# Splitting one attention product into high and low parts in a fused attention and expert kernel

## Chip, cores and metric

One core of one Trainium2 chip. The time is the device time of one execution in microseconds, the median of several runs.

## What is computed

For x of shape (8, 512, 128), in float32:

```python
def _L0_attn_ref(x, gamma, beta, w_qkv, w_out, b_out):
    xn = (x - mean) / jnp.sqrt(var + EPS) * gamma + beta
    q, k, v = jnp.split(jnp.einsum('bnc,ck->bnk', xn, w_qkv), 3, axis=2)   # 4 heads of 32
    q = q * DIM_HEAD ** (-0.5)
    k = jax.nn.softmax(k, axis=1)
    context = jnp.einsum('bnhd,bnhe->bhde', k, v)
    out = jnp.einsum('bhde,bnhd->bnhe', context, q)
    return jnp.einsum('bnk,kc->bnc', out.reshape(b, n, 128), w_out) + b_out + x

x = x + _layernorm(_L0_attn_ref(_layernorm(x), ...))
x = x + _layernorm(_L0_ffn_ref(_layernorm(x), Wg, Wu, Wd))
# ffn: sum over 8 experts of (silu(x @ wg) * (x @ wu)) @ wd, hidden size 512
```

## The kernel before

A batch is 512 tokens of 128 channels. The expert part of a batch has 8 experts times 4 blocks of 128 hidden units, 32 **steps**. `body(b)` on every engine walks through the 32 steps of batch b: TensorE makes the gate product, the up product and the down product of three steps earlier (`LAG`); ScalarE the silu `gs` and the high part `h_hi` of h; VectorE `h = gs * up` and the low part `h_lo = h - h_hi`. Each product is float32 accuracy out of three fp32r matmuls of 512 columns (`products`, L1203 to L1206): high by high, low by high, high by low. Gate and up accumulators are three banks each, so a step's h may lag some steps.

The attention of the next batch c = b + 1 is threaded into those steps, and the first part of that of b + 2 too (its normalised rows `xh` and their transpose). Where each piece stands is a table written by hand: `PE_AT`, `DVE_AT`, `ACT_AT` and `POOL_AT` give the step on TensorE, VectorE, ScalarE and GpSimd, and on each engine a piece stands in front of that step's own work, in the middle, or at its end (`FRONT`, `MIDDLE`). Batch 0 has a prologue of its own and its body uses the `FIRST_` tables; batch 1's attention, made in body 0, uses other code (`first`). The engines run their queues in order and meet through semaphores.

The pieces around the change, in the body b for batch c = b + 1:

- step 1: the keys `kT`; step 2: their maximum, the exponentials `ET`, and `E_T`, a transpose within 32x32 blocks. SyncE stores this to DRAM and loads it back in another order (L458, L463) into `t_out_E`, in four loads.
- step 8 on TensorE: **A**, the product of the exponentials with `xh`: four float32 matmuls of 128 columns (L1249), `xh` stationary. It waits for the four loads alone.
- step 9: VectorE evicts A into `A_sb`, scaled by gamma (L897), ahead of that step's h. Just before it makes `erec`, the reciprocal of the exponentials' sum (L891). TensorE makes **B** from it behind that step's down product (L1255). Steps 10 and 11: M and G in the same way; step 12: the attention's output.
- step 6, at its end, on VectorE: `next_stats`, the mean and variance of the input of b + 2 (L860, L845, L856, L850, L852). GpSimd takes the power (`next_rstd`, L504, step 7) and makes `xh` of b + 2 (`next_xn`, L529, step 10, after A has read the old one).
- step 13 to 15: final statistics and scale of batch b - 1; GpSimd adds the residual into `res` (L541, step 15). Steps 16 and 17 on VectorE: transpose of `xh`, the sum `z` and its statistics.

There are 8 bodies; those with `nxt` (b < 6) prepare batch b + 2.

```python
                if at == "A":

                    pe.wait_ge(s_t_load["E"], c * 64)
                    for j in range(J):
                        last = pe.matmul(att_ps[:, 0:D].rearrange("p (i r) -> p i r", r=32), xh[:, j, :],
                                         from_group(t_out["E"][:, :])[:, j], start=(j == 0), stop=(j == J - 1))
                    last.then_inc(s_A_ps, 1)
```

Of the kernel before, what the change touches and what calls it, by code (L numbers as in the profile page):

```python
# [5 lines left out]
ALU = mybir.AluOpType  # L6
# [6 lines left out]
P = 128  # L13
# [17 lines left out]
             "x1_stats": 20, "x1n_T": 24, "next_xnT_lo": 28, "x1n_lo": 31}  # L31
FIRST_ACT = {"E_store": 5, "E_load": 8, "G": 14, "wk_hi": 18, "next_xnT": 26, "next_xnT_hi": 27, "x1n_hi": 30}
FIRST_POOL = {"y": 2, "yb": 6, "next_rstd": 10, "next_xn": 13, "z_rstd": 17, "x1": 17, "x1_rstd": 21}
PE_AT = {"kT": 1, "A": 8, "B": 9, "M": 10, "G": 11, "attn": 12}
DVE_AT = {"kmax": 2, "acc": 2, "E_T": 2, "next_stats": 6, "A": 9, "B": 10, "M": 11, "G": 12, "fin_stats": 13, "fin_scale": 14,
          "z_T": 13, "next_T": 16, "z": 17, "z_stats": 17, "x1_stats": 21, "next_xnT_lo": 23, "x1n_T": 24, "x1n_lo": 31}
ACT_AT = {"exp": 2, "G": 12, "next_xnT": 21, "next_xnT_hi": 22, "x1n_hi": 30}
POOL_AT = {"yb": 4, "next_rstd": 7, "next_xn": 10, "fin_rstd": 13, "fin_out": 15, "z_rstd": 18, "x1": 18, "x1_rstd": 21}

# [41 lines left out]
def build(nc, x, gamma, beta, w_qkv, w_out, b_out, Wg, Wu, Wd, out):  # L81
# [10 lines left out]
    with ctx:  # L92
# [75 lines left out]
        turned = ("x", "E", "x1n", "acc")  # L168
        t_blk = {k: sb(f"t_blk_{k}", [P, N]) for k in turned}
        t_out = {k: sb(f"t_out_{k}", [P, N]) for k in turned}  # L170
# [329 lines left out]
        def _(pool):  # L500
# [66 lines left out]
            def body(b, par, first, nxt, last):  # L567
                for s in range(STEPS):
                    for at, when in (FIRST_POOL if first else POOL_AT).items():
                        if when != s:  # L570
                            continue
                        if at == "fin_rstd":
                            power("fin", b, s_rstd["fin"], s_mv["fin"])
                        elif at == "fin_out":
                            finish(b - 1, 1 - par)
                        elif at == "next_rstd":
                            if nxt:
                                attention("x_rstd", b + 2, par)
# [67 lines left out]
        def _(act):  # L646
# [5 lines left out]
            def attention(at, c, par, first):  # L652
                if at == "next_xnT":
# [187 lines left out]
        def _(dve):  # L841
# [25 lines left out]
            def attention(at, c, par, first):  # L867
# [10 lines left out]
                if at == "wk_lo":  # L878
                    dve.wait_ge(s_wk_hi, 1)
# [320 lines left out]
        def _(pe):  # L1200
# [324 lines left out]
```

## Time and profile before

| | |
|---|---|
| median of 3 runs | 543.82 us (543.82 to 544.1) |
| span of the profiled execution | 541.9 us |
| busy: TensorE, its weight loads | 99%, 86% |
| busy: VectorE, ScalarE, GpSimd | 81%, 64%, 31% |

The profile is of one execution. Its span runs from the first to the last instruction, 541.9 us; its own time outside the span is not given apart from the runs, and the median lies 1.9 us above the span. A row of the timeline has start, duration, engine, line, operation, output <- inputs, the tile of TensorE used, and partitions x elements; "x8" merges eight in a row, and brackets give idle time and what ended it. PE is TensorE's matmuls, PEld its weight loads, DVE VectorE, ACT ScalarE, POOL GpSimd. Matmuls overlap, so their spacing and not their duration says what they cost; a float32 matmul shows as two records.

### The profile page before, as it was taken

The page shows a single profiled execution, that of the slowest core. Times are in us where ns is not written, and L with a number is a line of the kernel's source. Part 1 is how long each engine was busy: PE and PEld are TensorE (multiplying, and loading weights), DVE is VectorE, ACT ScalarE, POOL GpSimd, SP SyncE. Part 2 cuts the span into 40 slices and gives each one's busy share as a digit, 9 for nine tenths or more (in the row PEclk, how much of TensorE's full clock was granted, in tenths as well). Part 3 has the DMA queues.
Part 4 walks back from the last instruction along what each step waited for, and adds up shares of the span by engine and source line. Part 5 has one row for each costly group of instructions (what it writes and reads, how often), then busy time and mean ns, then how long its engine had stood idle before and what let it go on. Part 6 is the DMA issues. An engine that isn't in the chain of part 4 may idle for free.

```text
span 541.9 us, 8650 instructions
## 1 busy us (share of the span) xinstructions
PE 535.4 (99%) x2582; PEld 466.4 (86%) x2582; DVE 441.5 (81%) x965; ACT 348.7 (64%) x633; POOL 167.7 (31%) x217
## 2 busy tenths in 40 slices
PE   9999999999999999999999999999999999999996
PEld 6788888888888888888888888888888888888886
DVE  6896877899777997879977898688987799777866
ACT  5986877557674575855667576665767555655555
POOL 6797950217102280114602045021530016000101
PEclk9999999999999999999999999999999999999999
DMA  7253111120120201202102112021111110110000
GB/s 218 82 169 109 53 59 46 33 72 26 60 72 8 93 25 39 79 19 79 51 9 79 40 59 59 4 75 39 60 39 48 31 60 0 41 39 1 20 2 19
DMA packets 33797, 28.68 MB, mean 53 GB/s; under 512 B 3411, under 2 KB 25686, under 8 KB 33750
## 3 DMA queue, kind: packets, MB, share of 16 engines
q1 hardware_dynamic: 32736, 27.47, 16.1%
q10 hardware_dynamic: 1014, 0.66, 0.4%
q8 instruction: 20, 0.33, 0.3%
q14 instruction: 27, 0.22, 0.1%
HBM read 17.37 MB, written 10.75 MB: 52 GB/s over the span
## 4 chain that ended last, share of the span: by engine, by line
PE 98%; ACT 1%; issue 0%; DVE 0%; POOLq 0%; POOL 0%; DVEq 0%
PE acc_att_ps L1203 11%; PE acc_att_ps L1206 11%; PE acc_att_ps L1204 11%; PE gate_ps L1203 10%; PE gate_ps L1206 10%; PE gate_ps L1204 10%; PE up_ps L1203 10%; PE up_ps L1206 10%; PE up_ps L1204 10%; PE acc_att_ps L1249 1%; PE up_ps L1320 1%; ACT xh L792 0%; PE acc_att_ps L1264 0%; PE acc_att_ps L1261 0%; PE acc_att_ps L1255 0%; PE acc_att_ps L1435 0%
## 5 line engine op out<-in xcount | busy, mean ns | idle before, releaser
L730 ACT ACTIVATE gs<-gate_ps 128x512 f32<-128x512 f32 x255 | 152.1, 597 | 172.8 <-PE gate_ps L1206 170.9
L1006 DVE TENSOR_TENSOR h<-gs,up_ps 128x512 f32<-128x512 f32 x231 | 157.7, 683 | 76.5 <-PE up_ps L1206 66.9
L993 DVE TENSOR_TENSOR h_lo<-h,h_hi 128x512 fp32r<-128x512 f32 x231 | 171.9, 744 | 0.1
L707 ACT ACTIVATE h_hi<-h 128x512 fp32r<-128x512 f32 x231 | 144.0, 624 | 6.4 <-DVE h L1006 5.2
L1203 PE MATMUL gate_ps<-x1nT_hi,wg_hi 128*128 128x512 f32 (+1 forms) x254 | 98.4, 387 | 0.0
L1203 PE MATMUL acc_att_ps<-h_hi,wd_hi 128*128 128x512 f32 (+1 forms) x256 | 96.8, 378 | 0.0
L1206 PE MATMUL acc_att_ps<-h_lo,wd_hi 128*128 128x512 f32 (+1 forms) x256 | 96.8, 378 | 0.0
L1204 PE MATMUL acc_att_ps<-h_hi,wd_lo 128*128 128x512 f32 (+1 forms) x256 | 96.8, 378 | 0.0
L1204 PE MATMUL gate_ps<-x1nT_hi,wg_lo 128*128 128x512 f32 (+1 forms) x254 | 96.1, 378 | 0.0
L1206 PE MATMUL gate_ps<-x1nT_lo,wg_hi 128*128 128x512 f32 (+1 forms) x254 | 96.1, 378 | 0.0
L1203 PE MATMUL up_ps<-x1nT_hi,wu_hi 128*128 128x512 f32 (+1 forms) x254 | 96.1, 378 | 0.0
L1204 PE MATMUL up_ps<-x1nT_hi,wu_lo 128*128 128x512 f32 (+1 forms) x254 | 96.1, 378 | 0.0
L1206 PE MATMUL up_ps<-x1nT_lo,wu_hi 128*128 128x512 f32 (+1 forms) x254 | 96.1, 378 | 0.0
L510 POOL TENSOR_TENSOR rstd_fin<-mv_fin,expo 128x4 f32<-128x4 f32 (+1 forms) x9 | 8.6, 955 | 173.1 <-DVE mv_fin L845 140.3
L1206 PEld LDWEIGHTS acc_att_ps<-h_lo,wd_hi 128*128 128x128 f32 x256 | 48.4, 189 | 7.2
L1204 PEld LDWEIGHTS acc_att_ps<-h_hi,wd_lo 128*128 128x128 f32 x256 | 48.4, 189 | 6.8
L1203 PEld LDWEIGHTS acc_att_ps<-h_hi,wd_hi 128*128 128x128 f32 x256 | 48.4, 189 | 6.8
L1204 PEld LDWEIGHTS up_ps<-x1nT_hi,wu_lo 128*128 128x128 f32 x254 | 48.0, 189 | 6.8
L1203 PEld LDWEIGHTS up_ps<-x1nT_hi,wu_hi 128*128 128x128 f32 x254 | 48.0, 189 | 6.8
L1206 PEld LDWEIGHTS up_ps<-x1nT_lo,wu_hi 128*128 128x128 f32 x254 | 48.0, 189 | 6.8
L1206 PEld LDWEIGHTS gate_ps<-x1nT_lo,wg_hi 128*128 128x128 f32 x254 | 48.0, 189 | 6.7
L1204 PEld LDWEIGHTS gate_ps<-x1nT_hi,wg_lo 128*128 128x128 f32 x254 | 48.1, 189 | 6.0
(263 smaller groups left out, 555.3 us busy)
## 6 DMA issues: line engine op xcount, KB each, us to landing
w_raw<-in_L_ffn_Wg_dram SPq DMA_DIRECT2D x8, 256.0 KB, 3.2
w_raw<-in_L_ffn_Wu_dram SPq DMA_DIRECT2D x8, 256.0 KB, 3.0
w_raw<-in_L_ffn_Wd_dram SPq DMA_DIRECT2D x8, 256.0 KB, 3.3
x_in<-in_L_attn_x_dram SPq DMA_DIRECT2D x7, 256.0 KB, 2.9
t_dram_x1n<-t_blk_x1n SPq DMA_DIRECT2D x7, 256.0 KB, 2.0
t_out_x1n<-t_dram_x1n SPq DMA_DIRECT2D x28, 64.0 KB, 2.0
t_dram_acc<-t_blk_acc SPq DMA_DIRECT2D x7, 256.0 KB, 2.3
t_out_acc<-t_dram_acc SPq DMA_DIRECT2D x28, 64.0 KB, 2.1
```

The lines of the kernel that those rows point to most:

```text
L510: pool.tensor_tensor(rstd[k][:, 0, toks], mv[k][:, toks, 1], expo[:, toks], ALU.pow).then_inc(done, 1)
L707: act.activation(h_hi[s % NH][:, :], h_of(t, s)[:, :], ACT.Copy).then_inc(s_hhi, 1)
L730: act.activation(gs[q][:, :], gate_ps[q][:, :], ACT.Silu).then_inc(s_silu, 1)
L993: dve.tensor_tensor(h_lo[s % NH][:, :], h_of(t, s)[:, :], h_hi[s % NH][:, :].bitcast(F32), ALU.subtract).then_inc(s_hlo, 1)
L1006: dve.tensor_tensor(h_of(t, s)[:, :], gs[q][:, :], up_ps[q][:, :], ALU.mult).then_inc(s_h, 1)
L1203: pe.matmul(ps, w_h, x_h, start=start, stop=False)
L1204: pe.matmul(ps, w_l, x_h, start=False, stop=False)
L1206: return pe.matmul(ps, w_h, x_l, start=False, stop=stop)
L1249: last = pe.matmul(att_ps[:, 0:D].rearrange("p (i r) -> p i r", r=32), xh[:, j, :], from_group(t_out["E"][:, :])[:, j], start=(j == 0), st ...
L1320: pe.matmul(ps[:, 0:cols].rearrange("p (a b) -> p a b", b=P), warm[:, :], warm[:, :].rearrange("p (a b) -> p a b", a=1).to_broadcast([P, c ...
```

## The change

For batches 2 to 7, `xh` and the exponentials are split into high and low parts in fp32r, as the expert products are. A becomes four matmuls of 256 columns, `xh_hi` by the high and low exponentials side by side, and four of 128 columns, `xh_lo` by the high exponentials, accumulated onto the first 128 columns. The other 128 columns are added in the eviction, which becomes two VectorE instructions.

The new pieces: `E_hi` (ScalarE copy, end of step 6, waits for the four loads), `E_lo` (VectorE subtraction, end of step 6), `next_xh_hi` (ScalarE copy, end of step 15), `next_xh_lo` (GpSimd subtraction, step 17). `next_stats` moves from step 6 to step 8, `next_rstd` from 7 to 9, `next_xn` from 10 to 11. To make room, four tiles of the output stage (`t_blk` and `t_out` of the accumulator, `fn`, `res`) and the new `A_hi` go into `w_raw`, the weights' staging tile, free after batch 0; the prologue's `wvT_bd` goes into `zn`. `s_wk_hi` is renamed `s_hi` and also counts `xh_hi`.

```diff
-FIRST_ACT = {"E_store": 5, "E_load": 8, "G": 14, "wk_hi": 18, "next_xnT": 26, ...}
+FIRST_ACT = {"E_store": 5, "E_load": 8, "G": 14, "wk_hi": 18, "next_xh_hi": 24, "next_xnT": 26, ...}
+FIRST_POOL = {..., "x1_rstd": 21, "next_xh_lo": 25}
-DVE_AT = {"kmax": 2, "acc": 2, "E_T": 2, "next_stats": 6, "A": 9, "B": 10, ...}
+DVE_AT = {"kmax": 2, "acc": 2, "E_T": 2, "E_lo": 6, "next_stats": 8, "A": 9, "B": 10, ...}
-ACT_AT = {"exp": 2, "G": 12, "next_xnT": 21, "next_xnT_hi": 22, "x1n_hi": 30}
-POOL_AT = {"yb": 4, "next_rstd": 7, "next_xn": 10, "fin_rstd": 13, "fin_out": 15, "z_rstd": 18, ...}
+ACT_AT = {"exp": 2, "E_hi": 6, "G": 12, "next_xh_hi": 15, "next_xnT": 21, "next_xnT_hi": 22, "x1n_hi": 30}
+POOL_AT = {"yb": 4, "next_rstd": 9, "next_xn": 11, "fin_rstd": 13, "fin_out": 15, "next_xh_lo": 17, "z_rstd": 18, ...}
...
+        def E_part(i):
+            return E_parts[:, :].rearrange("p (b h q) -> p h b q", b=2, h=2)[:, i]
...
+                if at == "xh_lo":
+                    pool.wait_ge(s_hi, c)
+                    pool.tensor_tensor(xh_lo[:, :, :], xh[:, :, :], xh_hi[:, :, :].bitcast(F32),
+                                       ALU.subtract).then_inc(s_xh_lo, 1)
...
+                if at == "next_xh_hi":
+                    act.wait_ge(s_xh, c)
+                    act.wait_ge(s_A_ps, c - 1)
+                    act.activation(xh_hi[:, :, :], xh[:, :, :], ACT.Copy).then_inc(s_hi, 1)
+                if at == "E_hi":
+                    act.wait_ge(s_t_load["E"], c * 64)
+                    act.wait_ge(s_A_ps, c - 1)
+                    act.activation(E_part(0), two(t_out["E"][:, :]), ACT.Copy).then_inc(s_E_hi, 1)
...
+                if at == "E_lo":
+                    dve.wait_ge(s_E_hi, c - 1)
+                    dve.tensor_tensor(E_part(1), two(t_out["E"][:, :]), E_part(0).bitcast(F32),
+                                      ALU.subtract).then_inc(s_E_lo, 1)
...
-                        dve.tensor_scalar(A_sb[:, :], att_ps[:, 0:D], gb_cols[:, 0:1], None, ALU.mult).then_inc(s_A, 1)
+                        dve.tensor_scalar(two(A_hi), blocks_first(att_ps[:, 0:D]), gb_cols[:, 0:1], None, ALU.mult).then_inc(s_A, 1)
+                        dve.wait_ge(s_A, 2 * c - 2)
+                        dve.scalar_tensor_tensor(out=two(A_sb[:, :]), in0=blocks_first(att_ps[:, D:2 * D]), scalar=gb_cols[:, 0:1],
+                                                 in1=two(A_hi), op0=ALU.mult, op1=ALU.add).then_inc(s_A, 1)
...
+                if at == "A" and not first:
+                    pe.wait_ge(s_hi, c)
+                    pe.wait_ge(s_xh_lo, c - 1)
+                    pe.wait_ge(s_E_lo, c - 1)
+                    for j in range(J):
+                        pe.matmul(att_ps[:, 0:2 * D], xh_hi[:, j, :],
+                                  E_parts[:, :].rearrange("p (b x j r) -> p j x r b", b=2, j=J, r=32)[:, j],
+                                  start=(j == 0), stop=False)
+                    for j in range(J):
+                        last = pe.matmul(att_ps[:, 0:D], xh_lo[:, j, :],
+                                         E_part(0).rearrange("p b (a j r) -> p j a r b", j=J, r=32)[:, j],
+                                         start=False, stop=(j == J - 1))
+                    last.then_inc(s_A_ps, 1)
```

**TensorE, step 8 of body 1**, before and in the change:

```order
L1204 MATMUL acc_att_ps<-h_hi,wd_lo 128x512
L1206 MATMUL acc_att_ps<-h_lo,wd_hi 128x512
L1249 MATMUL acc_att_ps<-t_out_E,xh 128x128 x4
L1203 MATMUL gate_ps<-x1nT_hi,wg_hi 128x512
L1204 MATMUL gate_ps<-x1nT_hi,wg_lo 128x512
L1206 MATMUL gate_ps<-x1nT_lo,wg_hi 128x512
```

```order
L1245 MATMUL acc_att_ps<-h_hi,wd_lo 128x512
L1247 MATMUL acc_att_ps<-h_lo,wd_hi 128x512
L1292 MATMUL acc_att_ps<-E_parts,xh_hi 128x256 x4
L1296 MATMUL acc_att_ps<-E_parts,xh_lo 128x128 x4
L1244 MATMUL gate_ps<-x1nT_hi,wg_hi 128x512
L1245 MATMUL gate_ps<-x1nT_hi,wg_lo 128x512
L1247 MATMUL gate_ps<-x1nT_lo,wg_hi 128x512
```

The four float32 matmuls give way to four of 256 and four of 128 columns at the same place.

**VectorE, from the end of step 6 to h of step 9 of body 1**, before (`erec` is the reciprocal, `A_sb` A's eviction):

```order
L860 BN_STATS st_x<-x_in 128x6 x4
L845 BN_AGGR mv_x<-st_x 128x2 x4
L856 TENSOR_SCALAR nm_x<-mv_x 128x4
L850 TENSOR_SCALAR ve_x<-mv_x 128x4
L852 TENSOR_SCALAR ve_x<-mv_x 128x4
L1006 TENSOR_TENSOR h<-gs,up_ps 128x512
L993 TENSOR_TENSOR h_lo<-h,h_hi 128x512
L1006 TENSOR_TENSOR h<-gs,up_ps 128x512
L993 TENSOR_TENSOR h_lo<-h,h_hi 128x512
L891 RECIPROCAL erec<-esum 128x1
L897 TENSOR_SCALAR A_sb<-acc_att_ps,gb_cols 128x128
L1006 TENSOR_TENSOR h<-gs,up_ps 128x512
```

The same engine in the change, first from h of step 6 to h of step 8, then from there to the second eviction (`w_raw` is here the tile `A_hi`):

```order
L1047 TENSOR_TENSOR h<-gs,up_ps 128x512
L1034 TENSOR_TENSOR h_lo<-h,h_hi 128x512
L920 TENSOR_TENSOR E_parts<-t_out_E,E_parts 128x2x256
L1047 TENSOR_TENSOR h<-gs,up_ps 128x512
L1034 TENSOR_TENSOR h_lo<-h,h_hi 128x512
L1047 TENSOR_TENSOR h<-gs,up_ps 128x512
```

```order
L1034 TENSOR_TENSOR h_lo<-h,h_hi 128x512
L892 BN_STATS st_x<-x_in 128x6 x4
L877 BN_AGGR mv_x<-st_x 128x2 x4
L888 TENSOR_SCALAR nm_x<-mv_x 128x4
L882 TENSOR_SCALAR ve_x<-mv_x 128x4
L884 TENSOR_SCALAR ve_x<-mv_x 128x4
L927 RECIPROCAL erec<-esum 128x1
L934 TENSOR_SCALAR w_raw<-acc_att_ps,gb_cols 128x128
L936 SCALAR_TENSOR_TENSOR A_sb<-acc_att_ps,gb_cols,w_raw 128x128
L1047 TENSOR_TENSOR h<-gs,up_ps 128x512
```

The statistics moved past two steps' h and h_lo to stand directly ahead of the reciprocal; E_lo took their place, and the eviction has a second instruction.

**GpSimd, from the power for the final statistics on, body 1**, before and in the change:

```order
L510 TENSOR_TENSOR rstd_fin<-mv_fin,expo 128x4
L541 TENSOR_TENSOR res<-fn,x_0 128x512
L510 TENSOR_TENSOR rstd_z<-mv_z,expo 128x4
L529 TENSOR_SCALAR zn<-z,nm_z,rstd_z 128x128 x4
L562 TENSOR_TENSOR x_0<-zn,x_in 128x512
```

```order
L525 TENSOR_TENSOR rstd_fin<-mv_fin,expo 128x4
L556 TENSOR_TENSOR w_raw<-w_raw,x_0 128x512
L567 TENSOR_TENSOR xh_lo<-xh,xh_hi 128x512
L525 TENSOR_TENSOR rstd_z<-mv_z,expo 128x4
L544 TENSOR_SCALAR zn<-z,nm_z,rstd_z 128x128 x4
L581 TENSOR_TENSOR x_0<-zn,x_in 128x512
```

xh_lo stands right behind the residual addition (L541 before, L556 in the change).

## Rows read from the trace of the kernel before

**Rows 1.** The page, part 4: chain that ended last, share of the span by engine

```profile
PE 98%; ACT 1%; issue 0%; DVE 0%; POOLq 0%; POOL 0%; DVEq 0%
```

**Rows 2.** Timeline, TensorE matmuls, steps 8 and 9 of b = 1 (start us, us)

```profile
99.06 0.38 PE L1206 MATMUL up_ps<-x1nT_lo,wu_hi 128*128 128x512 f32 x1
...
99.92 1.05 PE L1249 MATMUL acc_att_ps<-t_out_E,xh 128*128 128x128 f32 x8
...
101.03 0.38 PE L1204 MATMUL gate_ps<-x1nT_hi,wg_lo 128*128 128x512 f32 x1
...
101.89 0.38 PE L1206 MATMUL up_ps<-x1nT_lo,wu_hi 128*128 128x512 f32 x1
...
102.76 0.38 PE L1255 MATMUL acc_att_ps<-A_sb,wqkv 128*128 128x128 f32 x2
```

**Rows 3.** Timeline, TensorE weight loads (PEld), the load of B

```profile
102.55 0.41 PEld L1255 LDWEIGHTS acc_att_ps<-A_sb,wqkv 128*128 128x128 f32 x2
```

**Rows 4.** Prologue, TensorE: timeline, and line L1388 (duration ns min/median/max)

```profile
6.60 0.28 PE L1388 MATMUL up_ps<-gb_cols,wqkv 128*128 128x1 f32 x2
...
L1388 PE MATMUL up_ps<-gb_cols,wqkv x2: 169/210/250, 6.6 to 6.6; 128*128 128x1 f32 x2
...
18.75 0.28 PE L1449 MATMUL up_ps<-x1nT_hi,wu_hi 128*128 128x256 f32 x1
...
19.76 0.28 PE L1450 MATMUL up_ps<-x1nT_hi,wu_lo 128*128 128x256 f32 x1
```

**Rows 5.** Timeline, VectorE, steps 5 to 9 of b = 1

```profile
96.58 0.69 DVE L993 TENSOR_TENSOR h_lo<-h,h_hi 128x512 fp32r<-128x512 f32 x1
97.19 0.87 DVE L860 BATCH_NORM_STATS2 st_x<-x_in 128x6 f32<-128x128 f32 x4
...
98.72 0.68 DVE L1006 TENSOR_TENSOR h<-gs,up_ps 128x512 f32<-128x512 f32 x1
...
100.52 0.69 DVE L993 TENSOR_TENSOR h_lo<-h,h_hi 128x512 fp32r<-128x512 f32 x1
101.12 0.16 DVE L891 RECIPROCAL erec<-esum 128x1 f32<-128x1 f32 x1
101.19 0.33 DVE L897 TENSOR_SCALAR A_sb<-acc_att_ps,gb_cols 128x128 f32<-128x128 f32 x1
...
102.35 0.69 DVE L1006 TENSOR_TENSOR h<-gs,up_ps 128x512 f32<-128x512 f32 x1 [0.82 <-PE up_ps L1206]
```

**Rows 6.** Timeline, prologue, weight loads and matmuls behind a wait

```profile
12.73 0.30 PEld L1334 LDWEIGHTS gate_ps<-M_sb,accT 128*128 128x128 f32 x2 [0.33 <-DVE M_sb L1121]
...
12.73 0.49 PE L1334 MATMUL gate_ps<-M_sb,accT 128*128 128x128 f32 x2
```

**Rows 7.** Who waited for whom: us in total, times, longest us

```profile
POOL rstd_x L504 <- DVE ve_x L852: 127.6, 5, 25.9
```

**Rows 8.** Timeline, ScalarE, step 7 of b = 1

```profile
96.89 0.60 ACT L730 ACTIVATE gs<-gate_ps 128x512 f32<-128x512 f32 x1 [0.75 <-PE gate_ps L1206]
```

**Rows 9.** Loads of E (tile t_out_E) for b = 1, then b = 3

```profile
L463 SPq DMA_DIRECT2D t_out_E<-t_dram_E x4: 318/432/433, 93.2 to 94.5; - x4
...
DMA to landing us min/median/max: 1.8/1.9/2.1
...
DMA to landing us min/median/max: 1.8/2.0/2.9
```

**Rows 10.** Timeline, VectorE and GpSimd (POOL), steps 15 to 18 of b = 1

```profile
116.70 1.41 DVE L993 TENSOR_TENSOR h_lo<-h,h_hi 128x512 fp32r<-128x512 f32 x1
...
118.62 0.68 DVE L993 TENSOR_TENSOR h_lo<-h,h_hi 128x512 fp32r<-128x512 f32 x1
...
123.73 0.68 DVE L993 TENSOR_TENSOR h_lo<-h,h_hi 128x512 fp32r<-128x512 f32 x1
...
116.27 1.28 POOL L541 TENSOR_TENSOR res<-fn,x 128x512 f32<-128x512 f32 x1 [1.24 <-DVE fn L964]
```

**Rows 11.** Timeline, weight load of down(17)'s third product

```profile
125.01 0.19 PEld L1206 LDWEIGHTS acc_att_ps<-h_lo,wd_hi 128*128 128x128 f32 x1
```

More of the change, by code:

```diff
@@ L31 @@
              "x1_stats": 20, "x1n_T": 24, "next_xnT_lo": 28, "x1n_lo": 31}
-FIRST_ACT = {"E_store": 5, "E_load": 8, "G": 14, "wk_hi": 18, "next_xnT": 26, "next_xnT_hi": 27, "x1n_hi": 30}
-FIRST_POOL = {"y": 2, "yb": 6, "next_rstd": 10, "next_xn": 13, "z_rstd": 17, "x1": 17, "x1_rstd": 21}
+FIRST_ACT = {"E_store": 5, "E_load": 8, "G": 14, "wk_hi": 18, "next_xh_hi": 24, "next_xnT": 26, "next_xnT_hi": 27, "x1n_hi": 30}
+FIRST_POOL = {"y": 2, "yb": 6, "next_rstd": 10, "next_xn": 13, "z_rstd": 17, "x1": 17, "x1_rstd": 21, "next_xh_lo": 25}
 PE_AT = {"kT": 1, "A": 8, "B": 9, "M": 10, "G": 11, "attn": 12}
-DVE_AT = {"kmax": 2, "acc": 2, "E_T": 2, "next_stats": 6, "A": 9, "B": 10, "M": 11, "G": 12, "fin_stats": 13, "fin_scale": 14,
+DVE_AT = {"kmax": 2, "acc": 2, "E_T": 2, "E_lo": 6, "next_stats": 8, "A": 9, "B": 10, "M": 11, "G": 12, "fin_stats": 13, "fin_scale": 14,
           "z_T": 13, "next_T": 16, "z": 17, "z_stats": 17, "x1_stats": 21, "next_xnT_lo": 23, "x1n_T": 24, "x1n_lo": 31}
-ACT_AT = {"exp": 2, "G": 12, "next_xnT": 21, "next_xnT_hi": 22, "x1n_hi": 30}
-POOL_AT = {"yb": 4, "next_rstd": 7, "next_xn": 10, "fin_rstd": 13, "fin_out": 15, "z_rstd": 18, "x1": 18, "x1_rstd": 21}
+ACT_AT = {"exp": 2, "E_hi": 6, "G": 12, "next_xh_hi": 15, "next_xnT": 21, "next_xnT_hi": 22, "x1n_hi": 30}
+POOL_AT = {"yb": 4, "next_rstd": 9, "next_xn": 11, "fin_rstd": 13, "fin_out": 15, "next_xh_lo": 17, "z_rstd": 18, "x1": 18, "x1_rstd": 21}
 BUSY = {"start": 8, "wqk": 2, "w": 3, "z": 2, "xn": 2}
@@ L143, in build @@
         erec = sb("erec", [P, 1])
+        E_parts = sb("E_parts", [P, 2 * N], F32R)
+        xh_hi = sb("xh_hi", [P, J, D], F32R)
+        xh_lo = sb("xh_lo", [P, J, D], F32R)
+        A_hi = w_raw[:, 4, 0:D]
         A_sb = sb("A_sb", [P, D])
@@ L168, in build @@
         turned = ("x", "E", "x1n", "acc")
-        t_blk = {k: sb(f"t_blk_{k}", [P, N]) for k in turned}
-        t_out = {k: sb(f"t_out_{k}", [P, N]) for k in turned}
+        t_blk = {k: w_raw[:, 0, :] if k == "acc" else sb(f"t_blk_{k}", [P, N]) for k in turned}
+        t_out = {k: w_raw[:, 1, :] if k == "acc" else sb(f"t_out_{k}", [P, N]) for k in turned}
         t_blk["z"] = t_blk["E"]
@@ L174, in build @@
         t_dram = {k: nc.dram_tensor(f"t_dram_{k}", [P, N], F32) for k in (*turned, "z")}
-        fn = sb("fn", [P, J, D])
-        res = sb("res", [P, J, D])
+        fn = w_raw[:, 2, :].rearrange("p (j d) -> p j d", j=J)
+        res = w_raw[:, 3, :].rearrange("p (j d) -> p j d", j=J)
         xnT_hi = sb("xnT_hi", [P, N], F32R)
@@ L186, in build @@
         qT_v = accT[:, :]
-        wvT_bd = fn[:, :, :]
+        wvT_bd = zn[:, :, :]
         Ek = t_out["E"][:, :].rearrange("p (j d) -> p j d", j=J)
@@ L272, in build @@
         s_kT_ps = sem("s_kT_ps")
-        s_wk_hi = sem("s_wk_hi")
+        s_hi = sem("s_hi")
         s_wk_lo = sem("s_wk_lo")
@@ L279, in build @@
         s_erec = sem("s_erec")
+        s_E_hi = sem("s_E_hi")
+        s_E_lo = sem("s_E_lo")
+        s_xh_lo = sem("s_xh_lo")
         s_A_ps = sem("s_A_ps")
@@ L410, in exchange, with blocks_first @@
                     for g in range(P // 32)]
+        def E_part(i):
+            return E_parts[:, :].rearrange("p (b h q) -> p h b q", b=2, h=2)[:, i]
+        def blocks_first(v):
+            return v.rearrange("p (x b) -> p b x", b=2)
         def plain(v):
@@ L583, in body @@
                                 attention("xn", b + 2, par)
+                        elif at == "next_xh_lo":
+                            if nxt:
+                                attention("xh_lo", b + 2, par)
                         elif not last:
@@ L661, in attention @@
                                        bias=gb_cols[:, 1:2], scale=gb_cols[:, 0:1]).then_inc(s_xnT, 1)
+                if at == "next_xh_hi":
[6 more added lines that the diff above has]
+                    act.activation(E_part(0), two(t_out["E"][:, :]), ACT.Copy).then_inc(s_E_hi, 1)
                 if at == "wk_hi":
-                    act.activation(wk_hi[:, :], wqkv[:, D:2 * D], ACT.Copy).then_inc(s_wk_hi, 1)
+                    act.activation(wk_hi[:, :], wqkv[:, D:2 * D], ACT.Copy).then_inc(s_hi, 1)
                 if at == "next_xnT_hi":
@@ L696, in stages @@
                         continue
-                    if at in ("next_xnT", "next_xnT_hi"):
+                    if at in ("next_xh_hi", "next_xnT", "next_xnT_hi"):
                         if nxt:
@@ L878, in attention @@
                 if at == "wk_lo":
-                    dve.wait_ge(s_wk_hi, 1)
+                    dve.wait_ge(s_hi, 1)
                     dve.tensor_tensor(wk_lo[:, :], wqkv[:, D:2 * D], wk_hi[:, :].bitcast(F32),
@@ L953, in finish @@
                     dve.wait_ge(s_down, c * STEPS + STEPS)
+                    dve.wait_ge(s_wlo, NW)
                     dve.transpose(grouped(t_blk["acc"][:, :]), by_group_of_acc(acc_ps[:, :])).then_inc(s_acc, 1)
@@ L1244, in attention @@
                              s_xnT_lo, c - 1).then_inc(s_kT_ps, 1)
-                if at == "A":
+                if at == "A" and not first:
[11 more added lines that the diff above has]
+                    last.then_inc(s_A_ps, 1)
+                elif at == "A":
                     pe.wait_ge(s_t_load["E"], c * 64)
@@ L1252, in attention @@
                 if at == "B":
-                    pe.wait_ge(s_A, c)
+                    pe.wait_ge(s_A, 2 * c - 1)
                     pe.matmul(att_ps[:, 0:D], wqkv[:, 2 * D:3 * D], A_sb[:, :], start=True, stop=True).then_inc(s_B_ps, 1)
```

## The prediction

> **What bounds the kernel now.** The chain that ended last is TensorE for 98% of the span [rows 1], so every nanosecond added to its stream, or any wait it is made to take, is paid in full, and work on other engines is free until TensorE waits for it. I then read TensorE around step 8 of the body b = 1, where the product A stands [rows 2]. A and what follows run without a gap: A starts at 99.92 and the second matmul of the next gate at 101.03, so A holds the stream for 101.03 - 99.92 - 0.22 (the first gate matmul, at the spacing of a 512-column one) = 0.89 us, eight passes of 0.11. A float32 matmul of 128 columns is two passes. B, the product that reads A_sb, starts at 102.76, its weight load at 102.55 [rows 3].
>
> What paces those passes? In the prologue a float32 matmul with one single column also runs as two passes, the second 0.28 - 0.17 = 0.11 after the first [rows 4]. So 0.11 us is the price of loading 128 columns of 4-byte weights, not of streaming columns. The fp32r matmuls of 256 columns, which have a weight load each too, go from 18.75 to 19.76 in nine spacings: 0.112 each.
>
> Last, VectorE in the same place [rows 5], where it evicts A. There A_sb is ready at 101.19 + 0.33 = 101.52, 1.03 us before B's weight load wants it. That slack is the number on which this change turns.
>
> **A on TensorE.** Removed: 8 passes at 0.112 = 0.89. Added: four fp32r matmuls of 256 columns at 0.112 [rows 4] = 0.45, and four fp32r matmuls of 128 columns. No row shows the last. Below, they cannot beat the weight load that the one-column row shows if fp32r weights load like float32 ones: 0.112. From the other side they may lose the fp32r rate and cost as much as a whole float32 product of 128 columns, 2 x 0.11 = 0.22. If the weight load did not bind they would be about half a 256-column matmul, 0.056. I take 0.112, the nearest row. A is then 8 x 0.112 = 0.89: no gain. The ends for A are -0.22 and +0.43 us.
>
> The Trainium skill, TensorE: Matmul & The Clock Gate, section LDWEIGHTS, puts a weight load at its columns over 1.2 GHz whatever the rows, which would be 107 ns for 128 columns. By that rule, and by the row, eight loads before and eight after make the product no shorter; its section Back-to-back issue gap would give 56 ns for an isolated 128-column matmul and by it alone A would shrink by about 0.22.
>
> **The wait at B, the main term.** Between the A product and B, VectorE used to evict A_sb almost at once, because the statistics of the next input stood in step 6. Now E_lo stands there and the statistics are behind step 8's h_lo, directly ahead of A's eviction. Worked out in the times of the body of b = 1:
> - h of step 8 needs the up product: its last matmul starts at 99.06 and lasts 0.38, ends 99.44 [rows 2]; one step later the same hop took 102.35 - (101.89 + 0.38) = 0.08 [rows 2, 5]. So h starts at 99.52.
> - h_lo follows 0.60 later (an operation of this size holds VectorE for 101.12 - 100.52), at 100.12; the statistics 0.61 after that (97.19 - 96.58), at 100.73. They hold VectorE for 98.72 - 97.19 = 1.53 [rows 5]: 102.26.
> - Reciprocal 0.07 (101.12 to 101.19), then the eviction of the high half 0.33: 102.33 to 102.66. The second eviction adds the other 128 columns and waits for the first: 0.04 for the hop, and 0.33 to 0.35: A_sb ready at 103.05, where it was 101.52.
> - B's weight load can then start at 103.09, against 102.55 [rows 3]. A weight load that waited is not hidden under an earlier matmul: in the prologue two passes behind such a wait took 0.49 [rows 6] where B's pair takes 0.38 [rows 2], 0.11 more. B thus begins at 103.20 instead of 102.76: a stall of 0.44 us.
>
> It happens wherever the statistics of the batch after next exist: five bodies, b = 1 to 5 [rows 7]. 5 x 0.44 = 2.2 us. The sixth changed A (b = 6) has none ahead of it and keeps its slack of 1.03, less 0.38 for the second eviction. The stall does not depend on what A costs: if A takes 0.43 more, TensorE gets to B at 103.19, just when A_sb is there. So the two are not added in these five batches; they hide each other. Behind the stall nothing piles up: h of step 9 starts 0.7 later than its up product allows, its h_lo ends at about 104.3, and step 10's products come 0.44 later than before, so VectorE is caught up by then.
>
> **E_hi and E_lo.** ScalarE has 0.75 idle ahead of the silu of step 7 [rows 8] and E_hi is an operation of the silu's size, 0.60, so it hides, if E has landed. The last of its four loads is issued at 94.5 and lands in up to 2.1: 96.6 [rows 9]. E_hi to 97.2, E_lo to 97.9, h of step 7 and h_lo of step 6 end at 99.1: 0.4 ahead of 99.52. In one batch the loads took up to 2.9 [rows 9]: 0.8 later, so h of step 8 would start 0.3 late and B stall by as much more. I add 0.3 once. A itself needs E_lo by 99.7 and gets it by 98.7 even then. xh_hi, one ScalarE copy in step 15, has an idle of that kind to itself and costs nothing.
>
> **xh_lo on GpSimd.** The row that speaks here is VectorE's h_lo at 116.70: 1.41 us instead of 0.68, ending 0.56 behind GpSimd's addition for the output (116.27 + 1.28 = 117.55) [rows 10]. xh_lo is such an operation and comes next on that queue. VectorE has been waiting and goes first, to 118.11; xh_lo then runs to 119.39, and the h_lo of 118.62 ends at 119.95, 0.65 late. From there to h_lo of step 17, at 123.73, VectorE has no idle to absorb this; that one would end at 125.06, and TensorE's weight load for it stands at 125.01 [rows 11]. With the 0.22 that a load leads its matmul this just fits: 0. If GpSimd gets in first, VectorE loses 1.28 and TensorE about 0.6 per batch. Ends: 0 and 3.0 us.
>
> The Trainium skill, SBUF — State Buffer, section Who interferes with whom, says that a VectorE operation with two SBUF inputs and a GpSimd operation reading SBUF block each other for a whole instruction, the first issued winning. The 1.41 row agrees.
>
> The moved buffers (accumulator transpose, residual, zeros for the prologue in zn) change no duration and no order: 0.
>
> **Sum.** 2.2 + 0.3 + 0 = 2.5 us. The profiled span is 541.9; the median of the runs is 543.82, 1.9 more, taken as fixed. 543.8 + 2.5 = **546.3 us**. Own range 545.3 to 547.4: the stall between 0.3 and 0.55 and the late load in none to three batches.
>
> **Rivals.** Differences under 0.2%, 1.1 us, are what a measurement of this kernel can't tell from none.
> - *128-column fp32r matmuls at the float32 price.* Adds nothing in five batches, 0.43 in the last: 546.7. For it: no row excludes it. Inside the forecast's range; chance 0.30, the forecast proper 0.38.
> - *GpSimd first.* xh_lo pushes VectorE by 1.28 before step 17 and TensorE waits there too: 546.3 + 5 x 0.6 = 549.3, part of it at 547.5 to 548.5. Against it: VectorE is already waiting when the lock falls free. 0.17.
> - *No wait at B.* If statistics or evictions overlapped more than their rows say, by 0.5 us or more, A_sb would be in time and only equal passes remain: 543.8 to 544.8. Against it: all rows repeat alike. 0.10.
> - *Faster.* The 128-column matmuls stream at 0.056, weight loads of fp32r being cheaper, and B does not wait: 6 x 0.22 = 1.3 less, 542.5. It decides only if A_sb is ready by 102.3, 0.7 us before my chain; the one-column row speaks against the first half, the VectorE chain against the second. 0.05.
>
> Chances: slower 0.38 + 0.30 + 0.17 = 0.85, same 0.10, faster 0.05. Range 544.7 to 548.6: it leaves out the faster case, most of "no wait", and the upper part of "GpSimd first".
>
> **What would show it.** VectorE: statistics directly ahead of A's eviction, A_sb ending at about 3.6 us behind the last up matmul of step 8. TensorE: an idle before B whose releaser is A_sb, 0.3 to 0.5 us in five batches, none in the sixth; A's eight passes 0.11 apart or, for the first rival, the last four 0.22 apart. h_lo near step 15 lengthened behind xh_lo, and no gap at step 20. I am wrong if B has no idle ahead of it, or if the time stays below 544.7.

## The result, and the profile after

The changed kernel takes 546.50 us (median of 5 runs, 546.37 to 547.03) where the kernel before takes 543.82 (5 runs, 543.59 to 544.10): ratio 1.0052, 95% interval 1.0041 to 1.0062. The forecast was 546.3, range 544.7 to 548.6. The profiled execution took 547.03 with a span of 545.2, against 541.9 before; spans of the other four runs are 544.6 to 544.9.

The page after, its first lines and part 4, which answers to [rows 1]:

```profile
span 545.2 us, 8705 instructions
...
PE 537.2 (99%) x2582; PEld 466.6 (86%) x2582; DVE 451.1 (83%) x977; ACT 354.7 (65%) x645; POOL 180.3 (33%) x223
...
PE 93%; DVE 3%; ACT 1%; DMA 1%; issue 1%; SPq 0%; POOLq 0%; POOL 0%; DVEq 0%; ACTq 0%
```

TensorE still fills nearly the whole span, but its share of the chain fell from 98% to 93%: for some stretches the end now hangs on VectorE, ScalarE and a transfer. The view of waits says where (who waited for whom: us in total, times, longest us):

```profile
ACT E_parts L693 <- DMA t_out_E<-t_dram_E: 3.7, 6, 1.6
PEld acc_att_ps L1310 <- DVE A_sb L936: 3.5, 5, 1.2
...
PE acc_att_ps L1310 <- DVE A_sb L936: 1.5, 5, 0.8
```

L1310 is the product B (L1255 before). It waits for A_sb in five bodies, as often as there are statistics of a batch after next [rows 7]. The timeline of TensorE in the body b = 1, beside [rows 2, 3] (start us, us, engine, line, and in brackets the idle time before with its releaser), matmuls and then the weight load of B:

```profile
99.54 0.38 PE L1247 MATMUL up_ps<-x1nT_lo,wu_hi 128*128 128x512 f32 x1
...
100.40 0.61 PE L1292 MATMUL acc_att_ps<-E_parts,xh_hi 128*128 128x256 f32 x4
100.84 0.56 PE L1296 MATMUL acc_att_ps<-E_parts,xh_lo 128*128 128x128 f32 x4
...
101.51 0.38 PE L1245 MATMUL gate_ps<-x1nT_hi,wg_lo 128*128 128x512 f32 x1
...
103.58 0.49 PE L1310 MATMUL acc_att_ps<-A_sb,wqkv 128*128 128x128 f32 x2 [0.18 <-DVE A_sb L936]
...
104.12 0.38 PE L1245 MATMUL gate_ps<-x1nT_hi,wg_lo 128*128 128x512 f32 x1
...
103.57 0.30 PEld L1310 LDWEIGHTS acc_att_ps<-A_sb,wqkv 128*128 128x128 f32 x2 [0.58 <-DVE A_sb L936]
```

A starts at 100.40 and the second gate matmul at 101.51: less its 0.22 that is 0.89 us, to the hundredth what eight float32 passes took. From A to B it is 3.18, where it was 2.84: 0.34. From B to the second gate matmul behind it is 0.54, where a B that did not wait takes 0.44: in the kernel before from 102.76 [rows 2] to the line below. That is another 0.10, the weight load that could not hide. Together 0.44 us.

```profile
103.20 0.38 PE L1204 MATMUL gate_ps<-x1nT_hi,wg_lo 128*128 128x512 f32 x1
```

VectorE in the same stretch of the changed kernel, beside [rows 5]:

```profile
97.67 0.68 DVE L920 TENSOR_TENSOR E_parts<-t_out_E,E_parts 128x512 fp32r<-128x512 f32 x1
...
99.99 0.69 DVE L1047 TENSOR_TENSOR h<-gs,up_ps 128x512 f32<-128x512 f32 x1 [0.44 <-PE up_ps L1247]
100.60 0.68 DVE L1034 TENSOR_TENSOR h_lo<-h,h_hi 128x512 fp32r<-128x512 f32 x1
101.20 0.86 DVE L892 BATCH_NORM_STATS2 st_x<-x_in 128x6 f32<-128x128 f32 x4
...
102.73 0.15 DVE L927 RECIPROCAL erec<-esum 128x1 f32<-128x1 f32 x1
102.80 0.33 DVE L934 TENSOR_SCALAR w_raw<-acc_att_ps,gb_cols 128x128 f32<-128x128 f32 x1
103.17 0.35 DVE L936 SCALAR_TENSOR_TENSOR A_sb<-acc_att_ps,gb_cols,w_raw 128x128 f32<-128x128 f32 x1
```

The statistics hold VectorE for 102.73 - 101.20 = 1.53 directly ahead of the two evictions. A_sb ends at 103.52, 3.60 behind the end of the last up matmul of step 8 (99.54 + 0.38).

**The whole difference.** The starts of A are 100.40, 165.86, 231.32, 297.44, 362.89 and 428.36: periods of 65.46, 65.46, 66.12, 65.45 and 65.47, where before every period is 65.02. That is 0.44 in four bodies and 1.10 in the body of b = 3. The remaining 0.48 (100.40 against 99.92) arose in the prologue, before any of the new operations had run. The sum is 4 x 0.44 + 1.10 + 0.48 = 3.3, the difference of the spans. In b = 3 the exponentials landed late: the last load took 3.2, in the other five bodies 2.0 to 2.1. ScalarE, VectorE and TensorE there:

```profile
229.10 0.63 ACT L693 ACTIVATE E_parts<-t_out_E 128x512 fp32r<-128x512 f32 x1 [1.57 <-DMA t_out_E<-t_dram_E]
...
229.76 0.69 DVE L920 TENSOR_TENSOR E_parts<-t_out_E,E_parts 128x512 fp32r<-128x512 f32 x1 [1.09 <-ACT E_parts L693]
...
232.77 0.86 DVE L892 BATCH_NORM_STATS2 st_x<-x_in 128x6 f32<-128x128 f32 x4
...
235.15 0.49 PE L1310 MATMUL acc_att_ps<-A_sb,wqkv 128*128 128x128 f32 x2 [0.83 <-DVE A_sb L936]
```

A starts at 231.32 here. The statistics start 1.45 behind it, in b = 1 only 0.80: 0.65 of delay, and TensorE waits 0.83 instead of 0.18, the same 0.65 more. This is one execution, the slowest of the five; what the late load cost in the others no profile shows.

### The profile page after: what moved, and what is told of

Its sections match the earlier page's. It is cut to its first block, busy times and chain, and to the rows that moved or that the text cites. A ratio compares the mean times of both kernels' runs of the same rounds, so it can differ in the third digit from the quotient of the medians.

```text
span 545.2 us, 8705 instructions
## 1 busy us (share of the span) xinstructions
PE 537.2 (99%) x2582; PEld 466.6 (86%) x2582; DVE 451.1 (83%) x977; ACT 354.7 (65%) x645; POOL 180.3 (33%) x223
## 4 chain that ended last, share of the span: by engine, by line
PE 93%; DVE 3%; ACT 1%; DMA 1%; issue 1%; SPq 0%; POOLq 0%; POOL 0%; DVEq 0%; ACTq 0%
PE acc_att_ps L1247 10%; PE acc_att_ps L1245 10%; PE acc_att_ps L1244 10%; PE gate_ps L1244 10%; PE gate_ps L1245 10%; PE gate_ps L1247 10%; PE up_ps L1245 10%; PE up_ps L1247 10%; PE up_ps L1244 10%; PE up_ps L1375 1%; DVE st_x L892 1%; DVE h_lo L1034 1%; DMA t_out_E<-t_dram_E 1%; PE acc_att_ps L1310 0%; DMA t_dram_E<-t_blk_E 0%
## 5 line engine op out<-in xcount | busy, mean ns | idle before, releaser
L1034 DVE TENSOR_TENSOR h_lo<-h,h_hi 128x512 fp32r<-128x512 f32 x231 | 176.9, 766 | 0.1
L519 POOL TENSOR_TENSOR rstd_x<-ve_x,expo 128x8 f32<-128x8 f32 x6 | 9.9, 1654 | 142.5 <-DVE ve_x L884 142.5
```

The lines of the kernel that those rows point to most:

```text
L519: pool.tensor_tensor(rstd["x"][:, :, :], ve_x[:, :, :], expo[:, :].rearrange("p (a j) -> p a j", j=J), ALU.pow).then_inc(s_rstd["x"], 1)
L1034: dve.tensor_tensor(h_lo[s % NH][:, :], h_of(t, s)[:, :], h_hi[s % NH][:, :].bitcast(F32), ALU.subtract).then_inc(s_hlo, 1)
```

## Experiments

The ratios are those to the kernel before, measured on the same chip (543.78 to 543.81 in all three groups of runs). "Period" is the time from one batch's A to the next.

**Statistics one step earlier** (stats_step7). The theory: the wait at B is made by the 1.53 us of statistics that stand between h_lo and A's evictions. The rival: the passes of A, or E_lo, are what costs.

```diff
-DVE_AT = {..., "E_lo": 6, "next_stats": 8, "A": 9, ...}
+DVE_AT = {..., "E_lo": 6, "next_stats": 7, "A": 9, ...}
```

> The change with the statistics of the input at the end of step 7 instead of 8. Theory (A_sb is late because the statistics stand behind h of step 8, which waits for its up product): they now fill the idle ahead of that h. Chain in the change's own times: statistics 99.47 to 101.0, h and h_lo to 102.2, both evictions to 103.0, B's weight load 103.04 against 103.03 when TensorE comes there. B waits 0 to 0.1 instead of 0.45 in five batches: 544.3 to 544.8. Rival (the added work on the engines or on shared ports costs the time wherever it stands): still 546.2 to 546.6.

544.96 us (544.63 to 545.69, 11 runs), ratio 1.0022 (1.0014 to 1.0031). Its waits:

```profile
PEld acc_att_ps L1310 <- DVE A_sb L936: 1.5, 2, 1.1
```

Two bodies wait instead of five: periods are 65.02, 65.27, 65.95, 65.02 and 65.02. The other three lose nothing at all. The two that still wait (b = 2 by 0.25, b = 3 by 0.93) are those in which VectorE had to wait for E: in b = 2 the last load is issued 5.0 us ahead of A and not 5.4 as in b = 1 (159.9 for 164.92, 94.5 for 99.90), in b = 3 a load lands after 3.0. Their sum, 1.18, agrees with the difference of the medians, 1.17. The median is 0.2 above the expected range, which had nothing for late exponentials.

**Statistics in the body before** (stats_before). The same work, at the end of step 31 of the body before, where nothing of this stretch waits behind it.

```diff
-DVE_AT = {..., "E_lo": 6, "next_stats": 8, "A": 9, ...}
+DVE_AT = {..., "E_lo": 6, "A": 9, ...}
...
                     stages(s, b, par, first, nxt, last, "end")
+                    if s == STEPS - 1 and b + 3 < B:
+                        dve.wait_ge(s_yb, b + 2)
+                        attention("x_stats", b + 3, 1 - par, False)
```

> The change with the statistics of batch c made at the end of step 31 of the body before (for batches 3 to 7), where VectorE has idle. Theory: nothing stands between h_lo of step 7 and A's evictions, A_sb is ready about 102.2 in the change's times, 0.8 ahead of B's weight load: no idle at B at all, also in a batch whose E lands late. 544.2 to 544.5, the rest over 543.8 being the start. Rival (added work costs wherever it stands): 546.2 to 546.6.

543.80 us (543.66 to 544.20, 11 runs), ratio 1.0001 (0.9992 to 1.0009): the whole loss is gone, the late batch's too. Period 65.02 in every body, and no wait of TensorE for A_sb. VectorE in b = 1, where B starts at 103.05:

```profile
101.26 0.35 DVE L934 TENSOR_SCALAR w_raw<-acc_att_ps,gb_cols 128x128 f32<-128x128 f32 x1
101.64 0.35 DVE L936 SCALAR_TENSOR_TENSOR A_sb<-acc_att_ps,gb_cols,w_raw 128x128 f32<-128x128 f32 x1
```

A_sb is ready at 101.99, 0.85 ahead of B's weight load at 102.84. All the added operations (E_hi, E_lo, xh_hi, xh_lo, the second eviction) are in this kernel, so where they stand they cost nothing. In b = 3 a load of E took 2.8 here too, and A_sb came only 0.1 later behind A (232.12 - 230.25 = 1.87, in b = 1 1.77). The median is 0.4 below the expected range: that had added the later start of the changed kernel's profiled execution, and the median does not contain it.

**One eviction** (one_eviction) and **the kernel before with the statistics in step 8** (before_stats8) split the wait into its two causes. one_eviction leaves the product of the high rows with the low exponentials out of A_sb.

```diff
-    dve.tensor_scalar(two(A_hi), blocks_first(att_ps[:, 0:D]), gb_cols[:, 0:1], None, ALU.mult).then_inc(s_A, 1)
-    dve.wait_ge(s_A, 2 * c - 2)
-    dve.scalar_tensor_tensor(out=two(A_sb[:, :]), in0=blocks_first(att_ps[:, D:2 * D]), ...
+    dve.tensor_scalar(two(A_sb[:, :]), blocks_first(att_ps[:, 0:D]), gb_cols[:, 0:1], None, ALU.mult).then_inc(s_A, 1)
...
```

> The change without the second eviction of A: the product of the high rows with the low exponentials is computed and not used. Theory: A_sb is ready 0.37 earlier, so B waits 0.07 instead of 0.45: 544.5 to 544.9. Rival (the statistics alone make the wait): about 546.3.

```diff
 # in the kernel before
-DVE_AT: "next_stats": 6      POOL_AT: "next_rstd": 7, "next_xn": 10
+DVE_AT: "next_stats": 8      POOL_AT: "next_rstd": 9, "next_xn": 11
```

> The kernel before with only the tables of the change: statistics in step 8, the power in 9, xh in 11. No splitting. Theory: A_sb ready at 102.66 in the times of before, B's weight load 102.70 against 102.55, B itself 0.05 later: 0.05 x 5, 543.9 to 544.3. Rival (the placement alone makes the loss): 545.5 or more.

one_eviction: 544.68 us (544.25 to 545.41, 11 runs), ratio 1.0017 (1.0008 to 1.0026); before_stats8: 544.08 (543.91 to 544.52, 11 runs), ratio 1.0004 (0.9995 to 1.0013). Their waits, one_eviction first:

```profile
PEld acc_att_ps L1307 <- DVE A_sb L934: 1.2, 5, 0.4
```

```profile
PEld acc_att_ps L1255 <- DVE A_sb L897: 1.0, 5, 0.2
```

Both periods are 65.08, 0.06 above 65.02 (in one_eviction 65.28 for b = 3). By them one_eviction should be 0.5 above before; its median is 0.9 above, with runs spread over 1.2. So the placement alone uses up the slack of 1.03 and goes 0.06 beyond it. The second eviction then adds 103.17 - 102.80 = 0.37, all of it exposed, to 0.44. Without the placement, in stats_before, the same eviction costs nothing. Neither has a price of its own.

**What a pass costs.** Three kernels, all on stats_before, where B does not wait: without the four low products (no_lo), the remaining four cut to 128 columns as well (hi_128), and the low products widened to 256 (lo_256). no_lo and hi_128 leave parts of A out; in hi_128 the second eviction adds what an earlier product left in those columns.

```diff
 # no_lo: this loop is left out
-    for j in range(J):
-        last = pe.matmul(att_ps[:, 0:D], xh_lo[:, j, :], E_part(0)..., start=False, stop=(j == J - 1))
 # hi_128: and in the other loop
-        pe.matmul(att_ps[:, 0:2 * D], xh_hi[:, j, :], E_parts[:, :]..., start=(j == 0), ...)
+        pe.matmul(att_ps[:, 0:D], xh_hi[:, j, :], E_part(0)..., start=(j == 0), ...)
 # lo_256: the low loop stays, with
+        last = pe.matmul(att_ps[:, 0:2 * D], xh_lo[:, j, :], E_parts[:, :]..., ...)
```

> The kernel with the statistics made in the body before, and A without its four products of xh_lo with the high exponentials (left out of A). Theory (a 4-byte weight load of 128 columns costs 0.112 whatever streams behind it): 4 x 0.112 x 6 = 2.7 less than 543.8, 541.1. Rival (a 128-column fp32r matmul costs its columns, 0.056, and the 256-column ones 0.17): 1.3 less, 542.5.

> As the one before, and the four remaining products of A narrowed from 256 to 128 columns (the high exponentials alone; the low ones are left out, the second eviction adds stale numbers). Theory (weight loads set the pace): same as with 256 columns, 541.1. Rival (columns set the pace): another 4 x 0.056 x 6 = 1.3 less.

> The kernel with the statistics made in the body before, and the four products of xh_lo widened from 128 to 256 columns, so that low by low is added too. Theory (weight loads set the pace): no change, 543.8. Rival (columns set the pace): 1.3 more, 545.1.

no_lo: 541.06 us (541.01 to 541.73, 4 runs), ratio 0.9953 (0.9938 to 0.9968). hi_128: 541.07 (541.02 to 541.31, 4 runs), ratio 0.9951 (0.9936 to 0.9966). lo_256: 543.81 (543.63 to 544.27, 10 runs), ratio 1.0002 (0.9992 to 1.0011). TensorE in b = 1, A and the second gate matmul behind it, of no_lo, then hi_128, then lo_256:

```profile
99.89 0.61 PE L1295 MATMUL acc_att_ps<-E_parts,xh_hi 128*128 128x256 f32 x4
100.55 0.38 PE L1248 MATMUL gate_ps<-x1nT_hi,wg_lo 128*128 128x512 f32 x1
```

```profile
99.99 0.55 PE L1295 MATMUL acc_att_ps<-E_parts,xh_hi 128*128 128x128 f32 x4
100.65 0.38 PE L1248 MATMUL gate_ps<-x1nT_hi,wg_lo 128*128 128x512 f32 x1
```

```profile
99.86 0.61 PE L1295 MATMUL acc_att_ps<-E_parts,xh_hi 128*128 128x256 f32 x4
100.31 0.61 PE L1299 MATMUL acc_att_ps<-E_parts,xh_lo 128*128 128x256 f32 x4
100.97 0.38 PE L1248 MATMUL gate_ps<-x1nT_hi,wg_lo 128*128 128x512 f32 x1
```

Four passes hold the stream for 100.55 - 99.89 - 0.22 = 0.44 with 256 columns, and for 100.65 - 99.99 - 0.22 = 0.44 with 128. Eight of 256 take 0.89. Whether a pass has 128 or 256 columns changes nothing here, and the number of passes everything: 0.11 each. The time agrees: 24 passes fewer made no_lo 2.72 us faster, 0.113 a pass. By that, the change saved nothing on TensorE, since it put eight passes in the place of eight. Each of these passes has a weight load of its own, so the three kernels show the price of a pass; that the load sets it, and not something else that comes once a pass, they do not show by themselves. The Trainium skill, TensorE: Matmul & The Clock Gate, section LDWEIGHTS, gives a formula by which a load of 128 columns takes 107 ns, an estimate, whatever the rows. These three kernels come near it, with 110 to 113 ns a pass.

**GpSimd's subtraction twice** (xh_lo_twice), on stats_before: it asks whether "just fits" was right, and what the rival "GpSimd first" would have cost. One more such operation behind xh_lo must push VectorE once more. It writes a spare tile and changes no result.

```diff
                     pool.tensor_tensor(xh_lo[:, :, :], xh[:, :, :], ..., ALU.subtract).then_inc(s_xh_lo, 1)
+                    if c > 2:
+                        pool.wait_ge(s_xh_lo, 2 * c - 5)
+                        pool.wait_ge(s_wlo, NW)
+                        pool.tensor_tensor(w_raw[:, 5, :]..., xh[:, :, :], ..., ALU.subtract).then_inc(s_xh_lo, 1)
...
-                    pe.wait_ge(s_xh_lo, c - 1)
+                    pe.wait_ge(s_xh_lo, 2 * c - 3)
```

> The kernel with the statistics made in the body before, and GpSimd's subtraction for xh_lo done a second time into a spare tile, in five bodies. Theory (each such operation holds back VectorE's next operation with two SBUF inputs, and h_lo of step 17 has only 0.1 us left to its weight load): z is held by about 0.6, and TensorE waits about 0.45 ahead of the third down product of step 17, in five batches: 545.6 to 546.4. Rival (VectorE has room left there): 543.8 to 544.2.

545.42 us (545.34 to 546.01, 7 runs), ratio 1.0030 (1.0019 to 1.0042). First GpSimd and VectorE in steps 15 to 18 of b = 1 in the changed kernel, beside [rows 10], and the weight load of [rows 11]:

```profile
117.62 1.40 DVE L1034 TENSOR_TENSOR h_lo<-h,h_hi 128x512 fp32r<-128x512 f32 x1
...
119.54 1.17 DVE L1034 TENSOR_TENSOR h_lo<-h,h_hi 128x512 fp32r<-128x512 f32 x1
...
125.15 0.68 DVE L1034 TENSOR_TENSOR h_lo<-h,h_hi 128x512 fp32r<-128x512 f32 x1
...
117.19 1.28 POOL L556 TENSOR_TENSOR w_raw<-w_raw,x 128x512 f32<-128x512 f32 x1 [1.23 <-DVE w_raw L1005]
118.43 1.74 POOL L567 TENSOR_TENSOR xh_lo<-xh,xh_hi 128x512 fp32r<-128x512 f32 x1
...
125.94 0.19 PEld L1247 LDWEIGHTS acc_att_ps<-h_lo,wd_hi 128*128 128x128 f32 x1
```

And the same place of xh_lo_twice:

```profile
117.63 1.73 POOL L567 TENSOR_TENSOR xh_lo<-xh,xh_hi 128x512 fp32r<-128x512 f32 x1
119.32 1.74 POOL L572 TENSOR_TENSOR w_raw<-xh,xh_hi 128x512 f32<-128x512 f32 x1
...
120.47 1.14 DVE L966 TENSOR_TENSOR z<-zn,yb 128x512 f32<-128x512 f32 x1
...
124.85 0.69 DVE L1039 TENSOR_TENSOR h_lo<-h,h_hi 128x512 fp32r<-128x512 f32 x1
...
125.58 0.19 PEld L1255 LDWEIGHTS acc_att_ps<-h_lo,wd_hi 128*128 128x128 f32 x1 [0.47 <-DVE h_lo L1039]
```

In the changed kernel xh_lo lengthens one h_lo from 0.68 to 1.17, and h_lo of step 17 ends at 125.83, 0.11 before its weight load. There is no wait. With the second subtraction another VectorE operation is lengthened (z, 1.14), the same h_lo ends at 125.54, and the load waits 0.47. The period becomes 65.35, 0.33 more in five bodies, 1.65 in all, and the median is 1.64 above before. The mechanism is thus shown by making it happen. The median is 0.2 below the expected range: the 0.47 is the idle time of the weight load, which otherwise runs ahead of its matmul, and TensorE's stream lost only 0.33 a body, where 0.45 had been expected. xh_lo and its repetition each lengthened one VectorE operation by 0.5 (1.17 for 0.68, and 1.14 where z takes 0.64 in the changed kernel) and no more, although they stand back to back. A reading that fits the times is that the waiting VectorE operation went in between them: h_lo and z each end 0.55 behind the end of the GpSimd operation that they met (119.91 behind 119.36, 121.61 behind 121.06). The Trainium skill, SBUF — State Buffer, section Who interferes with whom, has it that a VectorE instruction with two SBUF inputs contends with a GpSimd instruction that reads SBUF, for ports that only one of them can hold. The rows agree: a VectorE operation of 0.68 takes 1.17 behind xh_lo, and xh_lo, which met a waiting h_lo, takes 1.74 where the addition before it took 1.28.

**E later by a place in a queue** (late_E on the changed kernel, late_E_prev on stats_before). SyncE issues the loads of the accumulator ahead of those of E, so that E lands some 2 us later. It measures what late exponentials cost, with and without the statistics behind them.

```diff
+                    load_blocks("acc", b)
                     if not last:
                         load_blocks("E", b + 1)
-                    load_blocks("acc", b)
```

> The change with the four loads of E issued behind the four of the accumulator, about 1.8 us later. Theory (E_lo waits in VectorE's queue ahead of step 7's h, so everything behind it to A's evictions moves with E): E_lo ends about 100.1 in the change's times, A_sb 104.8, B waits 1.7 instead of 0.45 in five batches: 551.5 to 553.5. Rival (the wait at B has nothing to do with when E lands): 546.2 to 546.8.

> The same later loads of E, with the statistics made in the body before. Theory: VectorE has 1.53 us less between E_lo and A's evictions, A_sb about 103.2, B waits 0.15 to 0.3 in six batches and A up to 0.6 where E lands latest: 544.6 to 546. Rival: 543.8.

late_E: 558.16 us (557.85 to 558.45, 4 runs), ratio 1.0263 (1.0246 to 1.0280). late_E_prev: 550.70 (550.38 to 550.96, 4 runs), ratio 1.0126 (1.0110 to 1.0141). Both expectations were missed, by 4.7 us above their upper ends. ScalarE, VectorE and TensorE of late_E in b = 1:

```profile
98.97 0.63 ACT L693 ACTIVATE E_parts<-t_out_E 128x512 fp32r<-128x512 f32 x1 [2.88 <-DMA t_out_E<-t_dram_E]
...
99.63 0.69 DVE L920 TENSOR_TENSOR E_parts<-t_out_E,E_parts 128x512 fp32r<-128x512 f32 x1 [2.41 <-ACT E_parts L693]
...
100.47 0.68 PE L1292 MATMUL acc_att_ps<-E_parts,xh_hi 128*128 128x256 f32 x4 [0.43 <-DVE E_parts L920]
...
105.02 0.49 PE L1310 MATMUL acc_att_ps<-A_sb,wqkv 128*128 128x128 f32 x2 [1.47 <-DVE A_sb L936]
```

The step that both expectations missed is A's own wait, late_E first and then late_E_prev:

```profile
PE acc_att_ps L1292 <- DVE E_parts L920: 4.2, 6, 1.8
```

```profile
PE acc_att_ps L1295 <- DVE E_parts L920: 4.5, 6, 1.6
```

late_E was expected to wait at B only, late_E_prev at A only where E lands latest; A waited in all six bodies. In b = 1 of late_E, E_lo ends at 100.32, so A waits 0.43, and then B comes 4.55 behind A instead of 2.84, 1.71 late, which is what had been expected of B. What the pair shows is the difference between the two: 7.46 us, over five bodies 1.49 each. The statistics take 1.53. Between stats_before and the changed kernel the difference was only 2.70, since there most of the 1.53 went into VectorE's slack. Once E_lo is late, no slack is left and the statistics lie on the chain whole.

## Why the prediction was right

- **The bound, and A on TensorE**: right. A takes 0.89 before and after. lo_256 (0), hi_128 (0) and no_lo (0.113 less for each pass left out) show that the pass and not the column is paid. The rival of the float32 price falls with it, and so does the half of "Faster" by which a 128-column matmul would take 0.056. The time alone could not have refuted that rival: 546.5 lies between its 546.7 and the forecast's 546.3.
- **The wait at B**: right in place, count and size. Forecast about 3.6 from the up product to A_sb, measured 3.60; forecast 0.44 in five bodies, measured 0.44 in four and that plus a late load in the fifth; none in the sixth (431.19 - 428.36 = 2.83). One detail was put in the wrong place: the load that could not hide costs its 0.11 not ahead of B but behind it, with the same sum. The rival "no wait at B" is refuted, and stats_before, where it is gone, shows that this wait is the whole loss.
- **E_hi and E_lo**: the mechanism right, the term mis-sized. "One late batch adds 0.3" was 0.65: the forecast took the longest landing of the kernel before, 2.9 [rows 9], while in the profiled execution after it was 3.2 in the batch b = 3. That is 0.3 of what the term lacks; the rest is in its own sum, where 99.1 + 0.8 - 99.52 is 0.38 and not 0.3.
- **xh_lo on GpSimd**: right that it costs nothing, and near. By the forecast's figures h_lo of step 17 would have ended 0.05 behind the start of its weight load (125.06 for 125.01); it ended 0.11 ahead. The delay was 0.49, forecast 0.65. The rival "GpSimd first" did not happen; xh_lo_twice shows that a longer hold there does reach TensorE, with 0.33 a batch where the rival had 0.6.
- **The sum**: 2.5 forecast, 2.68 measured. In the profiled execution the periods give 2.86: 2.20 for the five waits and 0.66 for the late load. If the five waits are 2.20 in the median run too, 0.5 is left there for the late load, an estimate. The difference of the spans is 3.3, and 0.48 of that is in the prologue, for which no term stood. Nothing points to the change as its cause: the eight experiments in which E is not moved start their first A between 99.86 and 100.22, and seven of them have the change's prologue.

No kernel here that computes the whole of A beats the one before. stats_before, the change with its statistics moved, equals it.

## What to carry to other kernels

Splitting a float32 product into high and low parts gained nothing on TensorE here, because it took as many passes. With 4-byte weights of 128 columns a pass cost 0.11 us in these kernels with 128 and with 256 columns behind it, and a float32 pass with a single one did too [rows 4]. So count the passes before the columns. When operations are put ahead of one that TensorE waits for, add up everything between the last matmul that VectorE needs and the eviction, and set it against the slack: two additions that are each nearly free (0.06 and 0.00 here) can cost 0.44 together. A long operation that nobody in the stretch waits for, here 1.53 us of statistics, belongs where the engine has idle time, and moving it can cover late transfers as well.

## What was not expected of the hardware

- Issuing the loads of E behind another set of four cost 11.7 us on top of 546.5 in late_E.
- In the batch b = 3 E lands late in the profiles of before (2.9 us) and of after (3.2), and the same body is the one that loses most in stats_step7 and in both kernels with late loads. The runs don't show why this batch.
- The prologue can differ by half a microsecond between two executions of nearly the same instructions. TensorE at its start, before and then after:

```profile
5.03 0.36 PE L1347 MATMUL up_ps<-ident,wqkv 128*128 128x128 f32 x1
5.22 0.27 PE L1349 MATMUL up_ps<-ident 128*128 128x128 f32 x1
```

```profile
5.03 0.42 PE L1402 MATMUL up_ps<-ident,wqkv 128*128 128x128 f32 x1
5.24 0.42 PE L1404 MATMUL up_ps<-ident 128*128 128x128 f32 x1
...
7.08 0.28 PE L1443 MATMUL up_ps<-gb_cols,wqkv 128*128 128x1 f32 x2
```

The two matmuls of 128 columns take 0.36 and 0.27 before, 0.42 and 0.42 after, and the granted clock from 5 to 7 us is 1.00 in both profiles. By the one-column matmul the whole 0.48 is there (7.08 against 6.60 [rows 4]), and the first A keeps it. That is nearly a fifth of the 2.68 measured, and only a comparison of periods instead of spans keeps it out. What decides it the runs don't show.
